# V kept unsplit in DRAM and split a group ahead, X^T by pairs of batches, earlier loads, Wq and Wk by thirds

## The reference

```python
x = x + einsum('bct,bcd->bdt', x, w0[itok])             # x: 32 x 128 x 1024, w0: 200 x 128 x 128
q, k, v = x @ Wq.T, x @ Wk.T, x @ Wv.T                  # 1024 x 1024 each, 16 heads of 64
scores = (q * min(cond, 4)) @ k.T / 8, causal mask      # per batch and head, 128 x 128
out = (softmax(scores) @ v) @ Wo.T
return x + out
```

## Time and profile before

| | us |
|---|---|
| median of 3 runs | 1632.22 (1632.01 to 1632.38) |
| the profiled execution | 1630.67 |
| its span | 1629.4 |
| TensorE busy | 1595.2 |
| VectorE busy | 1068.2 |
| ScalarE busy | 808.7 |
| GpSimd busy | 662.3 |

### The profile page before, as it was taken

How to read it: one execution, slowest core, us unless ns; L and a number is a source line. 1 busy time by engine, 2 the same in 40 slices (tenths; PEclk the granted TensorE clock), 3 DMA queues, 4 the chain that set the end, 5 groups by cost and what they waited for, 6 DMA issues and landing times.

```text
span 1629.4 us, 22999 instructions
## 1 busy us (share of the span) xinstructions
PE 1595.2 (98%) x7810; PEld 1340.5 (82%) x7810; DVE 1068.2 (66%) x2072; ACT 808.7 (50%) x2199; POOL 662.3 (41%) x554
## 2 busy tenths in 40 slices
PE   8899999999899999999999999999999999999999
PEld 6678777778788888888888888888888888888887
DVE  6757656566377777777777777777777745555553
ACT  6545556454155555655655555555555632222221
POOL 2446546465033333333433333343333325555552
PEclk9999999999999999999999999999999999999999
DMA  8979999997974644654359645454643487445442
GB/s 294 351 233 305 316 316 322 289 295 238 307 302 174 233 181 150 224 192 158 122 163 287 254 146 198 149 191 146 213 149 111 162 316 291 161 163 178 164 161 84
DMA packets 171815, 353.99 MB, mean 217 GB/s; under 512 B 13234, under 2 KB 97458, under 8 KB 161458
## 3 DMA queue, kind: packets, MB, share of 16 engines
q1 hardware_dynamic: 171698, 352.52, 63.4%
HBM read 201.47 MB, written 150.99 MB: 216 GB/s over the span
## 4 chain that ended last, share of the span: by engine, by line
PE 79%; DMA 6%; SPq 6%; DVE 3%; issue 2%; POOL 2%; ACT 2%; ACTq 0%; DVEq 0%
PE p_PJ L636 19%; PE p_PJ L637 19%; PE p_PJ L638 18%; PE p_SC L637 4%; PE p_SC L636 4%; PE p_SC L638 4%; PE p_PV L636 2%; PE p_PV L637 2%; PE p_PV L638 2%; DMA t_wr<-w 2%; DMA at_scratch<-t_AT 2%; DMA t_WL<-wl_scratch 1%; SPq L1316 1%; PE p_LP L637 1%; PE p_LP L636 1%
## 5 line engine op out<-in xcount | busy, mean ns | idle before, releaser
L636 PE MATMUL p_PJ<-t_XH,t_WH 128*128 128x512 f32 x1008 | 395.5, 392 | 4.8 <-DMA t_WL<-wl_scratch 4.8
L637 PE MATMUL p_PJ<-t_XL,t_WH 128*128 128x512 f32 x1008 | 395.4, 392 | 0.0
L638 PE MATMUL p_PJ<-t_XH,t_WL 128*128 128x512 f32 x1008 | 392.9, 390 | 0.0
L1240 POOL TENSOR_TENSOR t_PTL<-t_PT,t_PTH 128x512 fp32r<-128x512 f32 x128 | 163.0, 1295 | 517.5 <-ACT t_PTH L952 517.5
L1011 DVE STREAM_TRANSPOSE t_PT<-t_PP 32x256 f32<-32x256 f32 x640 | 278.3, 435 | 11.5 <-POOL t_PP L1236 1.9
L947 ACT ACTIVATE t_PP<-t_PP,t_st 128x128 f32<-128x128 f32 x512 | 198.5, 390 | 50.3 <-DVE t_st L1132 50.1
L638 PEld LDWEIGHTS p_PJ<-t_XH,t_WL 128*128 128x128 f32 x1008 | 189.8, 188 | 40.8
L636 PEld LDWEIGHTS p_PJ<-t_XH,t_WH 128*128 128x128 f32 x1008 | 190.3, 189 | 36.4 <-issue 5.2
L637 PEld LDWEIGHTS p_PJ<-t_XL,t_WH 128*128 128x128 f32 x1008 | 190.8, 189 | 30.0
L952 ACT ACTIVATE t_PTH<-t_PT 128x512 fp32r<-128x512 f32 x128 | 73.8, 624 | 194.7 <-DVE t_PT L1011 194.7
L1236 POOL TENSOR_TENSOR t_PP<-t_PP,t_st 128x512 f32<-128x512 f32 x128 | 132.7, 1043 | 83.4 <-DVE t_st L1136 83.4
(11 more groups left out here) (253 smaller groups left out, 3599.7 us busy)
## 6 DMA issues: line engine op xcount, KB each, us to landing
t_XH<-xth_scratch SPq DMA_DIRECT2D x14, 2048.0 KB, 9.0
t_XL<-xtl_scratch SPq DMA_DIRECT2D x14, 2048.0 KB, 14.1
vh_scratch<-t_VOH SPq DMA_DIRECT2D x64, 256.0 KB, 5.5
vl_scratch<-t_VOL SPq DMA_DIRECT2D x64, 256.0 KB, 6.2
xth_scratch<-t_XH SPq DMA_DIRECT2D x16, 1024.0 KB, 5.3
xtl_scratch<-t_XL SPq DMA_DIRECT2D x16, 1024.0 KB, 7.8
t_VH<-vh_scratch SPq DMA_DIRECT2D x16, 1024.0 KB, 4.8
t_VL<-vl_scratch SPq DMA_DIRECT2D x16, 1024.0 KB, 8.2
```

Of the source, the lines that this page charges most:

```text
L636: pe.matmul(bank, lh, rh, start=first, stop=False, skip_group_check=goes_on)
L637: pe.matmul(bank, lh, rl, start=False, stop=False, skip_group_check=goes_on)
L638: return pe.matmul(bank, ll, rh, start=False, stop=last, skip_group_check=goes_on)
L1240: pool.tensor_tensor(PTL[:, u:u + 2], PT[:, u:u + 2], PTH[:, u:u + 2].bitcast(f32), ALU.subtract).then_inc(pool_pt, 1)
```

## The change

- **V**: one DRAM tensor `v_scratch` in place of two. A piece is stored as it is, from one of four slots of `t_VR`. In the opening and for the first piece of a pair ScalarE copies it there from PSUM (`act_v_out`); for the other three VectorE's gather writes there directly. The 64 subtractions into `t_VOL` and 42 of the 64 copies are gone. In the attention a group's V is loaded once into `t_VX` and split tile by tile into `VH`, `VL` by ScalarE and GpSimd (`v_split`): for group 0 at steps 17, 19, 21, 23, for the others at steps 46.5, 47.5, 62.5, 63.5 of the group before. PV waits for the tile's subtraction. `V_load` of group j waits until the last split of group j-1 is through. (`t_VX` lies where `t_XR` was before and `t_WEH` will be later.)
- **X^T**: `XH`, `XL` are laid out by pair of batches, chunk of D, column (`XHP`, `x_place`, `x_chunk`). A pair's store is one run of 8 KiB per partition instead of eight of 1 KiB; the moving operand of q and k is two runs of 256 columns.
- **Wv's sums**: chunk 2 goes to raw tile 0 and chunk 3 to tile 1, each load after the chunk two before it (`dve_TL` 4 and 8 instead of 4 and 12), due at steps 30 and 39 instead of 31 and 50, the work at 42 and 51 instead of 43 and 59.
- **Conditioning**: the batch's weights are loaded 32 steps ahead instead of 21. Two ScalarE copies and one VectorE subtraction of X^T are due 0.75 step later, the second sum of X is split at steps 6 and 7 instead of 2.5 and 3.5.
- **Wq and Wk**: `W_load` in three parts of 128, 128 and 256 columns, each with its own semaphore, instead of whole or in halves; the blocks q and k of a cell wait for their part. In the sync program `W_load` comes after `X_load` and `V_load` of the same time. The raw piece of Wq or Wk has two tiles.

```diff
@@ the order of the work
-            vh_ev.put(8 * n + 8, n)
-            vl_ev.put(8 * n + 8.75, n)
-            v_store.put(8 * n + 9.75, n)
+            v_ev.put(8 * n + 8, n)
+            v_store.put(8 * n + 9, n)
...
-            l0_w.put(p - 21, bb)
+            l0_w.put(p - 32, bb)
...
-            T_load.put((10, 13, 31, 50)[c], c)
+            T_load.put((10, 13, 30, 39)[c], c)
             for i in range(4):
-                t = (24, 33, 43, 59)[c] + i
+                t = (24, 33, 42, 51)[c] + i
...
-                S_high.put(t + (-1.25, 2.5, 9.5, 13.5)[i], (p, i))
-                S_low.put(t + (-0.25, 3.5, 10.5, 14.5)[i], (p, i))
+                S_high.put(t + (-1.25, 6, 9.5, 13.5)[i], (p, i))
+                S_low.put(t + (-0.25, 7, 10.5, 14.5)[i], (p, i))
...
-        W_load.put(T_ATT - 23.5, (0, 0))
-        W_load.put(T_ATT - 15.5, (1, 0))
-        W_load.put(T_ATT + 5, (1, 1))
+        for t, item in ((-19.75, (0, 0)), (-11.75, (1, 0)), (-11.5, (0, 1)), (-11.25, (1, 1)), (-1, (0, 2)), (4, (1, 2))):
+            W_load.put(T_ATT + t, item)
...
-            V_load.put(t0 + 9 if j == 0 else t0 - STEPS + 28, j)
+            V_load.put(t0 + 2.75 if j == 0 else t0 - STEPS + (28 if j == 1 else 0.25), j)
+            for u in range(GB):
+                v_split.put(t0 + 17 + 2 * u if j == 0 else t0 - STEPS + 46.5 + u + 14 * (u // 2), (j, u))
         t = T_ATT + STEPS * (NG - 1)
-        W_load.put(t + 57, (2, 0))
-        W_load.put(t + 64.5, (3, 0))
-        W_load.put(t + 65, (3, 1))
+        for d, item in ((57, (2, 1)), (57.25, (2, 2)), (64.5, (3, 1)), (64.75, (3, 2)), (75, (2, 0)), (75.25, (3, 0))):
+            W_load.put(t + d, item)
@@ TensorE
-            mm = three(PJ[bank_of[kind, item]][:], lh, ll, XH[z][:, d, :], XL[z][:, d, :], d == 0, d == DC - 1)
+            mm = three(PJ[bank_of[kind, item]][:], lh, ll, x_chunk(XHP, z, d), x_chunk(XLP, z, d), d == 0, d == DC - 1)
...
-                if c == 0 and u == 0:
-                    pe.wait_ge(l_V[j % 2], 32 * (j // 2 + 1))
+                if c == 0:
+                    pe.wait_ge(pool_vl, GB * j + u + 2)
@@ ScalarE, then GpSimd
+                for j, u in v_split(tick):
+                    act.wait_ge(l_V, 16 * (j + 1))
+                    if j < 2:
+                        act.wait_ge(pe_P, 7 * (NP - 2))
+                    else:
+                        act.wait_ge(pe_pv, 16 * (j - 1))
+                    act.activation(VH[j % 2][:, u, :], VX[:, u, :], ACT.Copy).then_inc(act_vh, 1)
...
+                for j, u in v_split(tick):
+                    pool.wait_ge(act_vh, GB * j + u + 1)
+                    pool.tensor_tensor(VL[j % 2][:, u, :], VX[:, u, :], VH[j % 2][:, u, :].bitcast(f32), ALU.subtract).then_inc(pool_vl, 1)
@@ the sync engine
             if c >= 2:
-                sp.wait_ge(dve_TL, (4, 12)[c - 2])
+                sp.wait_ge(dve_TL, 4 * (c - 1))
...
-            sp.dma_start(vh_d[half][g][:, cols], VOH[n % 2][:].bitcast(f32)).then_inc(s_V[n % 2], 16)
-            sp.dma_start(vl_d[half][g][:, cols], VOL[n % 2][:].bitcast(f32)).then_inc(s_V[n % 2], 16)
+            sp.dma_start(v_d[half][g][:, b * 512:(b + 1) * 512], v_slot(n)).then_inc(s_V[n % 4], 16)
...
-            cols = slice(0, 512) if n % 2 == 0 else slice(256 * part, 256 * part + 256)
+            cols = (slice(0, 128), slice(128, 256), slice(256, 512))[part]
```

More of the change, by code:

```diff
@@ L144, in cond_attention @@
             wl = sb("wl", [128, 128], f32r, early)
+        with nc.sbuf_tensor("t_VX", [128, GB, 512], f32) as tile:
+            VX = tile
         WEH = sb("WEH", [128, 4, 512], f32r)
@@ L185, in cond_attention @@
         l_p = [sem(f"load_qk{n}") for n in range(2)]
-        l_W = [sem(f"load_wq_wk{n}") for n in range(4)]
-        l_W_rest = [sem(f"load_wk_rest{n}") for n in range(2)]
+        l_W = [[sem(f"load_wq_wk{n}_{part}") for part in range(3)] for n in range(4)]
         l_W1 = sem("load_first_columns")
@@ L200, in cond_attention @@
         l_XL = [sem(f"load_xl{n}") for n in range(2)]
-        l_V = [sem(f"load_v{n}") for n in range(2)]
+        l_V = sem("load_v")
         l_y = [sem(f"load_y{n}") for n in range(2)]
@@ L205, in cond_attention @@
         s_xt = [sem(f"store_xt{n}") for n in range(2)]
-        s_V = [sem(f"store_v{n}") for n in range(2)]
+        s_V = [sem(f"store_v{n}") for n in range(4)]
         s_at = [sem(f"store_at{n}") for n in range(2)]
@@ L221, in cond_attention @@
         mask_at, exp_at, recip_at, norm_at, turn0_at, turn1_at, half_at, ptl_at, at_at = (At() for _ in range(9))
-        q_ev, ql_ev, kh_ev, kl_ev, vh_ev, vl_ev, v_store = (At() for _ in range(7))
+        q_ev, ql_ev, kh_ev, kl_ev, v_ev, v_store, v_split = (At() for _ in range(7))
         w_high, w_low = At(), At()
@@ L467, in x1_stores, with x_place, x_chunk @@
             return sum(x_slot(k) == z for k in range(B))
-        def x_cols(bb):
-            return slice(bb % GB * 128, bb % GB * 128 + 128)
+        XHP, XLP = ([t[:].rearrange("p d t -> p (d t)").rearrange("p (b d t) -> p b d t", b=2, d=DC) for t in ts] for ts in (XH, XL))
+        def x_place(tile, bb, chunks):
+            return tile[0][:, bb % GB // 2, chunks, bb % 2 * 128:bb % 2 * 128 + 128]
+        def x_chunk(tile, z, d):
+            return tile[z][:, :, d, :]
         opening_banks = [LP, PV[1], SC[1], PV[0], SC[0]]
@@ L492, in raw_wv @@
         def raw_wv(c):
-            return [TS[c == 1][:, n, :] for n in range(4)]
+            return [TS[c % 2][:, n, :] for n in range(4)]
         T_PLACE = (0, 1, 3, 2)
@@ L511, in v_operand @@
                 k, b = {0: (0, 0), 2: (1, 0), 5: (1, 1)}[i]
-                return tuple(t[:, 4 * k:4 * k + 4, x_cols(2 * p + b)] for t in (XH[0], XL[0]))
+                return tuple(x_place(t, 2 * p + b, slice(4 * k, 4 * k + 4)) for t in (XHP, XLP))
             s = S_ORDER[{1: 0, 3: 1, 4: 2, 6: 3}[i]]
@@ L1322, in sp_load_qk @@
                 sp.wait_ge(dve_TL, 16)
-            elif m < 16:
-                sp.wait_ge(dve_p, m)
             elif m == 16:
-                sp.wait_ge(dve_S, 4 * (NP - 2))
-                sp.wait_ge(s_V[0], 32 * 32)
-                sp.wait_ge(s_V[1], 32 * 32)
-            elif m >= 18:
+                for n in range(4):
+                    sp.wait_ge(s_V[n], 16 * 16)
+            elif m not in (1, 17):
                 sp.wait_ge(dve_p, m - 1)
@@ L1344, in sp_load_W @@
         def sp_load_W(n, part):
-            cols = slice(0, 512) if n % 2 == 0 else slice(256 * part, 256 * part + 256)
+            cols = (slice(0, 128), slice(128, 256), slice(256, 512))[part]
             for low in range(2):
-                if n == 0 and low == 0:
+                if n == 0 and low == 0 and part == 0:
                     sp.wait_ge(s_p, 32 * 16)
@@ L1352, in sp_load_W @@
                     sp.wait_ge(pe_P, 7 * (NP - 3) + 2 * n + low + 1)
-                elif n == 2 and low == 0:
+                elif n == 2 and part == 1 and low == 0:
                     sp.wait_ge(pe_q, 4 * NG)
-                elif n == 3 and part == 0 and low == 0:
+                elif n == 3 and part == 1 and low == 0:
                     sp.wait_ge(pe_k, 4 * NG)
                 to = (WH, WL)[low][n % 2][:, :, cols].bitcast(f32)
-                sp.dma_start(to, qk_half(n, low, cols)).then_inc(l_W_rest[n // 2] if part else l_W[n], 16)
+                sp.dma_start(to, qk_half(n, low, cols)).then_inc(l_W[n][part], 16)
         def sp_load_W1():
@@ L1510, in sp_program @@
                     sp_store_qk(m)
-                for n, part in W_load(tick):
-                    sp_load_W(n, part)
                 for _ in W1_load(tick):
@@ L1518, in sp_program @@
                     sp_load_V(j)
+                for n, part in W_load(tick):
+                    sp_load_W(n, part)
                 for P in at_at(tick):
```

150 lines of the change are left out of this document (67 added, 83 removed).

## The result

| | before | after |
|---|---|---|
| median of 4 runs, us | 1632.30 (1632.01 to 1632.93) | 1613.45 (1611.61 to 1616.50) |
| ratio, 95% interval | | 0.9886 (0.9869 to 0.9903) |
| the profiled execution | 1630.67 | 1616.50 |
| its span | 1629.4 | 1615.2 |

The kernel became 18.9 us faster. 29.0 were forecast, and the median lies 1.5 us beyond the upper end of the range, 1612. The profiled execution of the kernel after is the slowest of its four.

The account below looks back on a forecast made before the run. It took full DMA queues to bound the six slow pairs of the seven-product loop. Gains of 13.5 + 8.5 + 6.7 + 1.0 less 0.7 made 29.0 us, from 1632.22 to a median of 1603.2; range 1598 to 1612.

Parts of the forecast that it names:

- V's first load: Start of the attention: load queued behind a V store, ScalarE's copy waiting ahead of exp; nothing to 2 us, not summed.
- the middle of the attention: Around group 8: smaller Wq and Wk load bursts shorten waits for P^T's low half; 1.0 us gained, bounds -2 and 2.3.
- The loop of seven products: Middle six pairs of batches: storing V unsplit relieves full DMA queues; 13.5 us gained, bounds 0 and 14.4.
- Rival (b): Middle pairs of the loop: bound by the engines' order, not queues; 13.5 us not gained, 1617 us; chance 0.05.
- Wv's last chunk: First pair of the loop: chunk loaded earlier into the other raw tile; 8.5 of 10.0 us gained, bounds 6 and 10.
- Wq and Wk by thirds: First q block: smaller loads remove its wait and the half clock; 6.7 us gained, bounds 3 and 7.2.
- rival (a): Attention's start or last chunk of Wv: slow 512-byte rows land late; 3 to 7 us not gained, about 1608; chance 0.12.
- Splits in the attention: Attention cells: added ScalarE copies and GpSimd subtractions for V cost 0.7 us in all, bounds 0 and 13.
- Rival (c): 32 attention cells: GpSimd holds up VectorE; 12 us given back, 1615 us; chance 0.05.
- Rival (e): Attention cells: GpSimd's V split comes late, in front of P^T's low half; costs 66 us, 1669 us; chance 0.03.
- The moving operand in two runs: 3,072 q and k matmuls: operand as two runs of 256 columns; taken as 0, at most 31 us.
- rival (d): q and k matmuls: each two-run operand costs as two matmuls; 31 us given back, 1634 us; chance 0.03.

Follow-up runs that it names:

- Run 9: Kernel after with group 0's V splits later, Wq's and Wk's later parts loaded singly, and loads around both stalls spread further; 1598.62 us, ratio 0.9793.
- run 6: Kernel before with one line changed: conditioning weights loaded 32 steps ahead instead of 21; 1616.08 us, ratio 0.9890.
- (7): Kernel after with X^T stored in its old 1 KiB rows and each V piece stored twice; 1622.13 us.
- run 10: Kernel after with one line undone: conditioning weights loaded 21 steps ahead again; 1612.65 us.
- run 5: Kernel before with only X^T by pairs of batches added (8 KiB store rows); 1622.66 us, ratio 0.9931.
- (4): Kernel after with each V piece stored a second time in a tensor nobody reads; 1618.16 us.
- (8): Kernel before with the second sum of X split at steps 6 and 7 of a pair instead of 2.5 and 3.5; 1631.88 us.
- run 11: Kernel after with Wq's three parts loaded together ahead of Wk, first q block waiting for all of Wq, first k block for half of Wk; 1608.66 us.
- Run 1: Kernel after with group 0's four V splits at steps 28 to 31 instead of 17, 19, 21, 23; 1610.45 us, ratio 0.9861.
- Run 2: Kernel after with the first third of Wq's and Wk's second half loaded at step 100 instead of 75; 1606.25 us, ratio 0.9840.
- run 12: Kernel after with V splits of groups 1 to 15 moved just ahead of GpSimd's subtractions for P^T's low half; 1710.92 us.
- runs 3: Kernel after with group 0's V splits at steps 28 to 31 and Wq's and Wk's second half loaded one part at a time; 1601.99 us, ratio 0.9814.

## Why the prediction came out wrong

Two terms at the attention put the time outside the range: V's first load, taken as "nothing to 2 us", cost 7.4, and the middle of the attention, bounded at -2, lost 8.8. Run 9, without the two stalls, gains 14.8 us more. The largest term of the sum came out for a reason other than the one given.

**The loop of seven products: the size was right, the cause wrong.** All 14.4 us came (13.5 forecast), and that is luck: the change happened to carry the one line that gives most of them. The step that failed is "So in this stretch the queues bound it". Runs 6 and 7 show TensorE without a wait at a share of 1.00 and 0.99, at 329 and 326 GB/s, in the very stretch where before had 0.98 at 311. The capacity of 317 GB/s that I worked out from share and rate was no capacity. What bound the pairs was latency with an order behind it: GpSimd wants the weights of a batch, 64 KiB, 8 steps (6.8 us) after their place on SP. SP came to them some 6 us late (runs 6 and 10), the landing took another 5.8 us (median from 175 to 350 us, 3.3 in run 10), and GpSimd does nothing else meanwhile. So full queues do have a part, by way of slow issues and landings, but not as a limit of bytes per us. I had given that line one sentence. It is worth 13 us here by itself (run 6), X^T's rows 7 (run 5, where GpSimd still stands 61.1 us for the weights). In the kernel after, the pairs stay at 23.68 with V's bytes as before (4), with the short rows besides (7), and with the late load (10), so no one of them is needed there, and their gains don't add up. Whether V's halving alone would do was not tried. Rival (b), "the engines' order, not the queues", had half of the cause; its price was wrong, since the change itself altered the order that mattered. And the sign was in the page of the kernel before: its part 5 has GpSimd idle for 143.6 us for these weights. The second sum of X, which I named among the removed obstacles, gives nothing (8).

The Trainium skill (Perfetto Trace Analysis, Identifying the Most-Contended Engine) says that for DMA one should go by the use made of HBM and not by occupancy, which sixteen engines make misleading. This case's traces agree on the second half: shares of 0.98, 0.99 and 1.00 stand beside 311, 326 and 329 GB/s, and only the lowest of them goes with a loss. The rate would not have told the cause either: the same bytes in longer pairs are a lower rate.

**Wv's last chunk and the conditioning of the opening: right, as far as is tested.** 10.0 us were to be had in the first pair; the excess of 60 to 120 us fell by 8.9, against 8.5 forecast, and there is no half clock there. VectorE's wait for that chunk fell from 6.58 to 0.66 us. In run 6 the stands stay, and VectorE still waits 5.9 us for Wv, so the early weights are not what removes them; no run moves the chunk alone.

**Wq and Wk by thirds: the wait went, and a worse one came.** q opens with no wait, and 7.2 us are gained, a little over the 6.7 forecast. But less than half of that is due to the thirds: in run 11, where q waits for all of Wq, the two gaps cost 3.2 us and no half clock follows. The rest came with an earlier issue: SP reaches Wq's load 3.1 us after the last pair's opening (at 383.65) and not 6.4 us (at 409.06), where it stood for VectorE's low halves of V, 17.4 us from 375 to 412 us. That the edit to V's stores did this is the nearest reading, and no run shows it alone. The step that failed is the last sentence of that part, on ScalarE's copy for V: "nothing to 2 us". It cost 7.4 us (5.08 of stand and the half clock behind it), so that the net is nothing (7.6 us of excess became 7.8). I had seen that the copy stands in order ahead of exp, and then left the term out of the sum; I had counted V's load as issued at its step, 2.75, and not behind stores that the full queue lets go in 4 us and that must land first. Run 1 removes this stall by moving the copy, run 11 goes without it as the load is earlier, run 4 makes it grow with the traffic. This is rival (a), with another price and another victim: not q, but the second cell's scores by way of V.

**Middle of the attention: wrong by sign.** "Now the bursts are 3, 3 and 2 MiB. I take 1.0" counts the bytes of a burst and not what SP does between them. The parts due at steps 64.5 and 75 follow each other without a break since SP is behind; the output stores then wait for eight issues, 22.4 us. The 2.3 us of waits for P^T did go (0.5 is left), but 8.8 were lost at group 8, far outside my bound of -2. Run 2 shows it by moving two parts: 7.2 us back. The step that failed is that the term was sized by the size of the bursts, with nothing for the small stores queued behind them.

**Splits in the attention: right, and nearly free.** The excess of 500 to 800 us is 3.1 in both kernels. GpSimd's subtraction for V is slower than that for P^T in the same kernel:

```profile
L1237 POOL TENSOR_TENSOR t_PTL<-t_PT,t_PTH 128x512 fp32r<-128x512 f32 x128 | 163.0, 1294 | 392.8 <-ACT t_PTH L956 392.8
...
L1227 POOL TENSOR_TENSOR t_VL<-t_VX,t_VH 128x512 fp32r<-128x512 f32 x64 | 92.0, 1460 | 73.3 <-ACT t_VH L915 73.3
```

The mean hides two kinds: 24 of the 64 take 1727 to 1749 ns and the other 40 take 1282 to 1301. The 24 are the second ones of a couple, with VectorE's subtraction for the weights (`t_OL`) lying across both, the one with both inputs in SBUF that the prediction had named. One such place:

```profile
456.40 2.99 POOL L1227 TENSOR_TENSOR t_VL<-t_VX,t_VH 128x512 fp32r<-128x512 f32 x2 [1.50 <-ACT t_VH L915]
...
457.17 1.07 DVE L1101 TENSOR_TENSOR t_OL<-t_xr,t_OH 128x512 fp32r<-128x512 f32 x1
```

VectorE's takes 0.96 to 1.07 us there instead of 0.69, having begun during the first of GpSimd's two, and GpSimd's second takes 0.45 longer than the others. In run 12, where the subtraction for V stands at another place of the cell, none is longer than 1307 ns. So VectorE gets in between the two of GpSimd, which is what the prediction worked out by the rule, and k's split is not late: TensorE has no wait of this kind from 450 to 800 us. The Trainium skill (SBUF — State Buffer, Who interferes with whom) has VectorE and GpSimd lock each other out for a whole instruction where both need the shared port; these durations agree with it. Rival (c) is out. Rival (e) was no danger as the change is placed, but its mechanism is real and its price was set too low: 66 us for 32 cells, 94 measured with 30 (run 12). The splits begin late there, behind ScalarE's copies, so that the 0.49 us in hand save nothing, and the clock falls too.

**The moving operand in two runs: right.** The distance between q and k matmuls is 0.227 us before, after, and in run 5, which has this operand in the kernel before; rival (d) is out.

**The sum.** By the excess: 14.4 + 8.9 + 7.2 + 2.4 = 32.9 to the good, 7.4 + 8.8 + 1.8 to the bad, which leaves 14.9; the spans differ by 14.2. Without the two stalls, and with the loads around them spread further, the change is worth what I said it could be at most: run 9 comes to 1598.6, and the lower end of my range was worked out as 1598 with all waits gone. The 1.8 us lie before 20 us, where the profiled execution of the kernel after has 3.4 us of half clock. It is scatter: runs 3, 7 and 12 have it too, runs 1, 2, 4, 9, 10 and 11 have not, and their first 20 us differ by little or nothing.

## What to carry to other kernels

A full DMA queue is not yet a bound: before you blame bytes, look at which small transfer an in-order engine stands for, and try to issue that one earlier; one such line gained as much here as the whole change did. When a copy is moved into a later stage, ask of each one when its load can be issued at the earliest, counting the stores that must have landed and the time that issuing takes on a full queue, and put the copy behind the work that TensorE waits for. Keep long rows of load issues apart, so that small stores with a buffer waiting for them get in between.
